# A decoder layer on one core: experts on tiles of 256 slots with stationary split weights, and one logarithm-and-exponential piece fewer in the attention

## The reference

```python
x = x + attention(layernorm(x))          # 16 heads, width 64 each for Q, K, V and the gate G
#   W = (1e-4 + cdist(Q, K)) ** -2 ;  W = W / (1e-4 + W.sum(-1))
#   H = G * (W @ V) ;  H @ W_out + b_out
x = x + cross_attention(layernorm(x), ctx)   # 16 heads, 77 keys, masked softmax
# experts on z = layernorm(x):
#   y = rmsnorm(z) ; top 2 of 8 experts by y @ gate_w ; softmax over the two
#   h = silu(y @ W1[e]) * (y @ W2[e])    # 256 -> 704, twice
#   out = h @ W3[e]                      # 704 -> 256
#   x = x + z + sum over the two experts of weight * out
```

## Time and profile before

| | before |
|---|---|
| time, median of 3 (us) | 1433.6 (1432.44 to 1435.71) |
| profiled execution: time, span (us) | 1438.0, 1436.2 |
| mean granted clock of PE | 0.957 |
| PE busy | 1293.2 us, 90% |
| DVE busy | 1131.8 us, 79% |
| ACT busy | 1036.1 us, 72% |
| POOL busy | 681.1 us, 47% |

### The profile page before, as it was taken

How to read it: one execution, slowest core, us unless ns; L and a number is a source line. 1 busy time by engine, 2 the same in 40 slices (tenths; PEclk the granted TensorE clock), 3 DMA queues, 4 the chain that set the end, 5 groups by cost and what they waited for, 6 DMA issues and landing times.

```text
span 1436.2 us, 23659 instructions
## 1 busy us (share of the span) xinstructions
PE 1293.2 (90%) x7065; PEld 862.1 (60%) x7066; DVE 1131.8 (79%) x1707; ACT 1036.1 (72%) x882; POOL 681.1 (47%) x516
## 2 busy tenths in 40 slices
PE   5899999999999999999997946999992999999995
PEld 4545554555455455545553714888872888888884
DVE  6988988898889889988988473788877767666672
ACT  1699999999999999999999921333332465656552
POOL 5456556665665665566555052333331244434441
PEclk9999999999999999999999768999995999999998
DMA  5000000000000000000000034122220144323322
GB/s 155 2 14 16 30 15 29 15 22 22 16 28 15 29 15 29 15 29 15 22 15 23 7 113 131 52 66 61 63 98 18 27 132 115 75 51 93 93 37 73
DMA packets 68830, 67.25 MB, mean 47 GB/s; under 512 B 6752, under 2 KB 61280, under 8 KB 68768
## 3 DMA queue, kind: packets, MB, share of 16 engines
q1 hardware_dynamic: 61504, 56.91, 12.4%
q0 software_dynamic: 7296, 9.97, 4.1%
HBM read 49.03 MB, written 19.92 MB: 48 GB/s over the span
## 4 chain that ended last, share of the span: by engine, by line
PE 50%; ACT 19%; issue 15%; DVE 12%; DMA 2%; POOL 1%; DVEq 0%; POOLq 0%; ACTq 0%; SPq 0%
ACT wts L1581 11%; PE ps_s L853 10%; PE ps_s L582 8%; PE ps_o L878 7%; PE ps_o L598 5%; PE ps_p L493 4%; PE ps_o L671 4%; ACT wts L1583 4%; DVE wts L1053 4%; PE ps_s L704 2%; PE ps_p L866 2%; PE ps_s L732 2%; ACT L1578 1%; PE ps_o L689 1%; PE ps_s L484 1%
## 5 line engine op out<-in xcount | busy, mean ns | idle before, releaser
L1053 DVE TENSOR_SCALAR wts<-ps_s,k 128x1024 f32<-128x1024 f32 x240 | 296.9, 1279 | 55.9 <-PE ps_s L582 52.5
L1760 POOL TENSOR_TENSOR v_aug<-v_aug,wts 128x1024 f32<-128x1024 f32 x96 | 232.4, 2421 | 228.0 <-DVE v_aug L1042 227.6
L598 PE MATMUL ps_o<-wts,head_rows 128*64 128x512 f32 x1024 | 249.0, 610 | 3.6 <-ACT wts L1583 3.6
L1581 ACT ACTIVATE wts<-wts,eps_d 128x2048 f32<-128x2048 f32 (+1 forms) x96 | 246.0, 2562 | 0.2
L1575 ACT ACTIVATE wts<-wts 128x4096 f32<-128x4096 f32 (+1 forms) x80 | 230.1, 2931 | 22.1 <-DVE wts L1061 19.1
L1583 ACT ACTIVATE wts<-wts 128x2048 f32<-128x2048 f32 (+1 forms) x96 | 238.4, 2484 | 3.0
L582 PE MATMUL ps_s<-q_hi,k_hi 64*128 64x512 f32 x512 | 122.8, 473 | 34.0 <-DVE wts L1053 17.8
L598 PEld LDWEIGHTS ps_o<-wts,head_rows 128*64 128x64 f32 x1024 | 63.3, 137 | 128.0 <-issue 117.6
L1042 DVE TENSOR_TENSOR v_aug<-v_aug,wts 128x1024 f32<-128x1024 f32 x96 | 126.5, 1318 | 6.5 <-ACT wts L1583 6.1
L878 PE MATMUL ps_o<-wts 128*128 x456 | 112.2, 388 | 0.7 <-DVE wts L1496 0.7
L582 PEld LDWEIGHTS ps_s<-q_hi,k_hi 64*128 64x128 f32 x512 | 49.2, 185 | 103.4 <-DVE wts L1053 62.4
(11 more groups left out here) (279 smaller groups left out, 2920.5 us busy)
## 6 DMA issues: line engine op xcount, KB each, us to landing
wts<-in_w SPq DMA_DIRECT2D x16, 704.0 KB
raw<-in_w_in SPq DMA_DIRECT2D x64, 128.0 KB, 2.2
h_t<-o_raw SPq DMA_DIRECT2D x16, 512.0 KB, 2.7
head_rows<-h_t SPq DMA_DIRECT2D x16, 512.0 KB, 4.3
wts<-in_w SPq DMA_DIRECT2D x8, 640.0 KB
acc<-wts SPq DMA_DIRECT2D x17, 128.0 KB, 1.9
wts<-in_x SPq DMA_DIRECT2D x2, 1024.0 KB, 5.8
wts<-in_x SPq DMA_DIRECT2D x1, 2048.0 KB, 9.3
```

Of the source, the lines that this page charges most:

```text
L598: mm = pe.matmul(ps_o[r, t], v_pair[:, b, r], wts[:, h, b, t], start=b == 0, stop=b == SB - 1)
L1053: dve.tensor_scalar(wts[:, h, b, :], ps_s[:, h, :], k2[:, 2 * b + h:2 * b + h + 1], 0.0, ALU.add, ALU.max).then_inc(S_.max_ok, 1)
L1581: act.activation(chunk(start, end), chunk(start, end), ACT.Ln, bias=eps_d[:, 0:1]).then_inc(S_.ln_ok, 1)
L1760: pool.tensor_tensor(acc_w[:, 0], acc_w[:, 0], wts[:, 0, b], ALU.add).then_inc(S_.add_ok, 1)
```

## The change

**Attention.** LOGS joins blocks 2 and 3 into one piece, so ACT runs four activations of 4096 elements a partition for blocks 2 to 7 and two pairs of 2048 for blocks 0 and 1; `rows_inverse` stands behind the joined piece.

**Experts.** A tile has 256 slots (TT), so there are 2, 2, 2, 3, 4, 2, 2 and 3 tiles, 20 in all, run one after the other. The weights' parts become the stationary operand (128 columns of a weight) and the turned y, 256 slots, moves. The products then come out with the hidden width on partitions, so h is not turned: `turn_h` and its copies go. A tile has 66 products for up and gate in three steps (g = 0, 1: two 128-wide pieces of the width each; g = 2: the fifth piece, and the last 64 of up and gate together), and 36 for down: h and W3 are also split into two parts (three products each), where before there was a single f32 product. All have 256 moving columns. ACT makes the high parts of h (`high_hidden`) and W3 (`high_down`), DVE the low parts (`low_hidden`, `low_down`). The weights' parts have one buffer, renewed in three pieces behind the steps of the tile before. `weigh_slots` is 768 wide a part in place of 640; its second half, PE's sum (`slot_weights`) and `read_slot_weights` stand inside tiles 0 and 1. POOL reads and writes two halves per tile; k_step shares a buffer with o_raw (o_step).

```diff
-LOGS = ((0, 1), (1, 2), (2, 3), (3, 4), (4, 6), (6, 8))
+LOGS = ((0, 1), (1, 2), (2, 4), (4, 6), (6, 8))
...
+ET = NT + E
+ES = 2 * ET
+TT = 2 * P
...
+        y_hi, y_lo = (v[:].rearrange("p (a c t) -> p a c t", a=2, c=DC) for v in (q_hi, q_lo))
...
+            def turn_in(k, n):
+                for q in (S_.yg_even, S_.yg_odd):
+                    pe.wait_ge(q, 16 * (k + 1))
+                if n >= 1:
+                    pe.wait_ge(S_.ytt_ok, 2 * k)
+                for half in range(2):
+                    for c in range(DC):
+                        mm = pe.transpose(ps_o[:, c * TT + half * P:c * TT + (half + 1) * P], y_in[:, half, c * P:(c + 1) * P], ident)
+                mm.then_inc(S_.yt2_mm, 1)
+            def hidden(k, out, weights):
                 for c in range(DC):
...
+                    y = [v[:, bass.ds(k & 1, 1), c].rearrange("p a t -> p (a t)") for v in (y_hi, y_lo)]
+                    w_hi, w_lo = (w(c) for w in weights)
+                    for n, (w, y_part) in enumerate(((w_hi, y[0]), (w_lo, y[0]), (w_hi, y[1]))):
+                        mm = pe.matmul(out, w, y_part, start=n == c == 0, stop=n == 2 and c == DC - 1)
+                return mm
...
+            def up_gate(k, g, n):
+                if g == 0:
+                    pe.wait_ge(S_.ytt_ok, 2 * k + 2)
+                pe.wait_ge(S_.wlo_ok, W_PIECES * k + g + 1)
+                if n >= 1:
+                    pe.wait_ge(S_.hm_ok, W_PIECES * (k - 1) + g + 1)
+                if g < 2:
+                    for j in range(2):
+                        for kind in range(2):
+                            out = ps_s[:, g, kind * HALF + j * TT:kind * HALF + (j + 1) * TT]
...
+                else:
+                    for kind in range(2):
+                        hidden(k, ps_p[:, kind * HALF:kind * HALF + TT], [lambda c, w=w: w[:, kind, c] for w in w_fifth])
+                    mm = hidden(k, ps_p[:, TT:2 * TT], [lambda c, w=w: w[:, c].rearrange("p k n -> p (k n)") for w in w_both])
...
+            def down(k, n):
+                pe.wait_ge(S_.hlo_ok, 2 * k + 2)
+                pe.wait_ge(S_.w3l_ok, k + 1)
+                if n >= 1:
+                    pe.wait_ge(S_.o_ok2, 2 * k)
...
+                        w_hi, w_lo = (w3_short if j == NC - 1 else [w[:, j] for w in w3_long])
+                        for m, (h, w) in enumerate(((h_hi, w_hi), (h_hi, w_lo), (h_lo, w_hi))):
+                            mm = pe.matmul(out, h, w, start=at == m == 0, stop=m == 2 and at == NC - 1)
+                mm.then_inc(S_.w3_mm, 1)
...
+            def expert_tile(k, n, last=False):
+                up_gate(k, 0, n)
+                if not last:
+                    turn_in(k + 1, n + 1)
+                if n == 1:
+                    slot_weights()
+                up_gate(k, 1, n)
                 if n >= 1:
-                    turn_h(i - 1, 1 - par, n == 1)
-                pe.wait_ge(S_.e_in, count)
-                pe.wait_ge(S_.ytt_ok, 2 * i + 2)
-                up_gate(i, par, 0, n == 0)
-                up_gate(i, par, 1, n == 0)
-                if not last:
-                    if n >= 2:
+                    if n == 1:
                         pe.wait_ge(S_.wslot_ok, 3)
-                    turn_in(i + 1, 1 - par, k + par)
-                if n >= 1:
-                    down(i - 1, 1 - par, slot_of(i - 1), n == 1)
+                    down(k - 1, n - 1)
+                up_gate(k, 2, n)
...
+                dve.tensor_copy(hi, ps_o[:, 0:HALF]).then_inc(S_.ytt_ok, 1)
+                dve.wait_ge(S_.ytt_ok, 2 * k + 1)
+                dve.tensor_tensor(lo, ps_o[:, 0:HALF], hi.bitcast(F32), ALU.subtract).then_inc(S_.ytt_ok, 1)
...
+            def gated(k, g, n):
+                dve.wait_ge(S_.silu_ok, W_PIECES * k + g + 1)
+                if n >= 1:
+                    dve.wait_ge(S_.hlo_ok, 2 * (k - 1) + (2 if g == 2 else 1))
+                if g < 2:
+                    dve.tensor_tensor(h_all[:, 2 * g:2 * g + 2].rearrange("p n t -> p (n t)"), s_up[g], ps_s[:, g, HALF:],
+                                      ALU.mult).then_inc(S_.hm_ok, 1)
+                else:
+                    dve.tensor_tensor(h_all[:, 4], s_up[2][:, 0:TT], ps_p[:, HALF:HALF + TT], ALU.mult)
+                    dve.tensor_tensor(h_all[DEL:P, 5], s_up[2][DEL:P, TT:], ps_p[DEL:P, TT:2 * TT], ALU.mult).then_inc(S_.hm_ok, 1)
...
+            def low_hidden(k, part):
+                dve.wait_ge(S_.hh_ok, 2 * k + part + 1)
+                hi, lo = (h_four, h_two)[part]
+                dve.tensor_tensor(lo, h_all[:, 4 * part:min(4 * part + 4, NC)], hi.bitcast(F32), ALU.subtract).then_inc(S_.hlo_ok, 1)
+            def expert_tile(k, n, last=False):
+                slot = slot_of(k)
                 if not last:
-                    slot = slot_of(i + 1)
-                if n >= 1:
-                    copy_h(i - 1, 1 - par, n - 1)
+                    slot_next = slot_of(k + 1)
+                gated(k, 0, n)
                 if not last:
-                    low_parts(i + 1, 1 - par, slot, 0, DC)
-                gated(i, par, 0, n)
+                    copy_in(k + 1)
+                    low_parts(k + 1, slot_next, 0)
+                if n == 1:
+                    read_slot_weights()
+                gated(k, 1, n)
                 if not last:
-                    low_parts(i + 1, 1 - par, slot, DC, 2 * DC)
-                gated(i, par, 1, n)
+                    low_parts(k + 1, slot_next, 1)
+                if n == 0:
+                    weigh_slots(1)
+                low_hidden(k, 0)
+                gated(k, 2, n)
+                low_down(k, slot)
+                low_hidden(k, 1)
                 if not last:
-                    copy_in(i + 1, 1 - par, n + 1)
+                    low_parts(k + 1, slot_next, 2)
...
-                    if c == 3 and not first:
+                    if c == 2 and not first:
                         rows_inverse(n - 1)
...
+                else:
+                    act.activation(s_up[2][:, 0:TT], ps_p[:, 0:TT], ACT.Silu)
+                    act.activation(s_up[2][DEL:P, TT:], ps_p[0:DEL, TT:2 * TT], ACT.Silu).then_inc(S_.silu_ok, 1)
...
+            def high_parts(k, slot, g, n):
+                if n >= 1:
+                    act.wait_ge(S_.ug_mm, W_PIECES * (k - 1) + g + 1)
+                raw12 = w12[:, bass.ds(slot, 1)].rearrange("p s k c n -> p (s k) c n")
+                if g < 2:
+                    high = act.activation(w_wide[0][g], raw12[:, :, :, g * TT:(g + 1) * TT], ACT.Copy)
+                else:
+                    act.activation(w_fifth[0], raw12[:, :, :, 4 * P:5 * P], ACT.Copy)
+                    high = act.activation(w_both[0].rearrange("p c k n -> p k c n"), raw12[:, :, :, 5 * P:], ACT.Copy)
+                high.then_inc(S_.whi_ok, 1)
...
+            def high_down(k, slot, n):
+                if n >= 1:
+                    act.wait_ge(S_.w3_mm, k)
+                raw3 = w3_sb[:, bass.ds(slot, 1)].rearrange("p s n d -> p (s n) d")
+                act.activation(w3_long[0], raw3[:, 0:NC - 1], ACT.Copy)
+                act.activation(w3_short[0], raw3[DEL:P, NC - 1], ACT.Copy).then_inc(S_.w3h_ok, 1)
+            def high_hidden(k, part, n):
+                act.wait_ge(S_.hm_ok, W_PIECES * k + (3 if part else 2))
+                if n >= 1:
+                    act.wait_ge(S_.w3_mm, k)
+                act.activation((h_four, h_two)[part][0], h_all[:, 4 * part:min(4 * part + 4, NC)], ACT.Copy).then_inc(S_.hh_ok, 1)
...
+            def copy_out(k, n):
+                act.wait_ge(S_.w3_mm, k + 1)
                 act.wait_ge(S_.wslot_ok, 3)
-                act.activation(o_sb[:, par], ps_o[:, HALF:HALF + D], ACT.Copy, scale=w_slot[:, bass.ds(i, 1)]).then_inc(S_.o_ok2, 1)
...
+            def expert_tile(k, n, last=False):
+                slot = slot_of(k)
+                if not last:
+                    slot_next, count = slot_of(k + 1), count_of(k + 1)
+                silu(k, 0, n)
+                if not last:
                     act.wait_ge(S_.e_in, count)
-                    if not (isinstance(i, int) and i <= 1):
...
+                    high_parts(k + 1, slot_next, 0, 1)
+                silu(k, 1, n)
                 if not last:
-                    slot, count = slot_and_count(i + 1)
+                    high_parts(k + 1, slot_next, 1, 1)
                 if n >= 1:
-                    copy_h(i - 1, 1 - par, n - 1)
+                    copy_out(k - 1, n - 1)
+                high_hidden(k, 0, n)
+                silu(k, 2, n)
+                high_down(k, slot, n)
+                high_hidden(k, 1, n)
                 if not last:
-                    high_parts(i + 1, 1 - par, slot, count, 0, DC)
...
+            def fetch_tile(k):
+                for half in range(2):
+                    fetch(k, half, 1)
+            def put_tile(k, first=False):
+                for half in range(2):
+                    put(k, half, first)
+            fetch_tile(1)
```

(33 more changed lines are left out.)

352 lines of the change are left out of this document (125 added, 227 removed).

## The result

| | before | changed |
|---|---|---|
| time, median (us) | 1434.03 (4 runs, 1432.44 to 1435.71) | 1446.41 (4 runs, 1444.29 to 1448.37) |
| ratio, 95% interval | | 1.0075, 1.0061 to 1.0090 |
| profiled execution: time, span | 1438.0, 1436.2 | 1444.29, 1442.0 |

The prediction was 1424, faster; the time rose by 12.4 us.

What follows compares the result with a forecast made beforehand. PE was taken to bound the experts; in the attention ACT's own work tied with the loop through ACT, DVE and PE. Experts -24.1 and attention +14.6 gave -9.5, so 1433.6 became 1424 us, range 1405 to 1441.

Steps and rivals of the forecast that it cites:

- The attention's term: Attention: joining blocks 2 and 3 delays DVE's add and lengthens the loop through ACT, DVE and PE; +14.6 us.
- the experts' term: Experts, end to end: 20 tiles of 256 slots at 12.9 us, plus waits at both ends; 24.1 us less.
- +1.15, in 13 of the 15 periods: Attention: us added to each period between pairs by the late add of block 2; first and last counted at 0.
- Rival C: Attention: slack absorbs the later add and ACT's saving of 6.3 us comes through, giving 1403; chance 0.15.
- with slack, since it reads three tiles ahead and writes three behind: Experts, POOL: its round of two reads and two writes, 12.5 to 13.2 us, was taken to have slack.
- rival D: Experts: DVE or POOL, not PE, sets a tile's pace at 13.6 us, giving 1438; chance 0.12.
- first product: Start of the experts: PE's first product waits for both halves of y, at 1116.7 instead of 1112.97.
- The tables of slots: Ahead of PE's wait for the first read: a few DVE instructions, counted at nothing, under 2 us if not covered.
- the first two tiles and the third's first step: Start of the experts: PE's work, slots' sum and waits, including 5.8 us for the slots' weights; 37.0 us.
- 16 tiles at 12.9: Middle of the experts: PE sets the pace, with 102 products of 0.118 us, turns and borders per tile.
- the last `down`: End of the experts: after a wait of 4.8 us, 4.25 us and 1 more at the lower clock.
- Rival B: Experts, PE: weight loads aren't hidden at 256 columns; 1440 at 0.126 us a product, 1459 at 0.135; chance 0.13.

Runs made afterwards that it cites:

- logs_alone: The kernel before the change with only the joined logarithm and exponential piece for blocks 2 and 3 added; 1452.76 us, 1.0117 of the kernel before.
- one_list_copy: The changed kernel with POOL copying the token list of both tile halves in one instruction instead of two; 1435.99 us, 1.0011 of the kernel before.
- logs_undone: The changed kernel with the six separate logarithm and exponential pieces restored, so only the experts differ from before; 1427.70 us, 0.9956 of the kernel before.

## Why the prediction was wrong

The sum was -24.1 for the experts and +14.6 for the attention. Measured apart it is -6.9 and +18. The attention's term held in mechanism; the experts' term failed.

**The attention: right in mechanism, too small.** "+1.15, in 13 of the 15 periods": 13 periods rose by 1.18 to 1.20. The first is as it was (49.01, before 48.96), as forecast. The last, counted at 0, rose by 0.97 (50.09, before 49.12). In the last pair ACT gives back 0.41, as forecast. Together that is 16.2 us, and so the traces have it, from the first table load to the end of the last Exp: 784.15 in place of 767.99. The medians say 18.1 and 18.7; the interval of logs_alone, 14.5 to 19.2, holds 16.2 as well, so the medians' excess can be noise. Rival C is out.

**The experts: the step that failed** is "with slack, since it reads three tiles ahead and writes three behind". Reading ahead hides a delay once; it doesn't shorten a round. The estimate in the same sentence, 12.5 to 13.2, was near the measured 13.50 and already above PE's 12.9 at its upper end. I noted that and let the slack excuse it. This was rival D, at 13.6 us a tile and 1438, given 0.12. The own work of the two others was forecast rightly: ACT 8.9 and DVE 10.6 us a tile, measured 140.17/16 = 8.8 and 165.90/16 = 10.4. Against the trace of the changed kernel, term by term:

- first product, 3.8 forecast for the second half's read: 3.4, for from the first read's issue to the first product it is 8.17 (1120.38 to 1128.55) where it was 4.78. The tables of slots, counted at nothing, put that read 0.8 later: 9.65 behind the start of the routing (1110.73), before 8.86.
- the first two tiles and the third's first step, 37.0 forecast: 35.4. PE's wait for the slots' weights was 5.24, forecast 5.8.
- 16 tiles at 12.9: 220.5 us, 13.78 each, 14.1 us more. Of these 0.1 a tile is PE's own: a product takes 0.120, the upper of the two scalings, not 0.118. Of the other 12.5, 8.7 are waits of PE: for POOL's round, and for the late landings under a weight load, which the sum didn't have at all. The last 3.8 are slower products around these waits (in the 15 us from the longest on, 1329 to 1344, the granted clock is 0.89). one_list_copy got 10.4 back.
- the last `down`, 5.25 forecast: 8.6, since in this trace all of it and not the first part ran at the low clock; its wait 5.66 for 4.8.
- the tiles behind the 16, up to that wait: 0.4 more than forecast; from the last `down` to the end 20.4 for 19.6.

These add up to 18.3 us, which takes the forecast's -24.1 to -5.8; the two traces, from the start of the routing to the end, give 331.3 in place of 336.9, so -5.6. logs_undone's median says -6.9.

**Rival B** (loads not hidden at 256 columns) is out: 0.120 is what 352 columns scaled with a fixed cost gave. The load just covered, by the rule of the Trainium skill, "TensorE: Matmul & The Clock Gate", section "LDWEIGHTS (loading the stationary operand)", is not excluded by that: the trace agrees so far as PE's load queue is busy 12.74 of 13.00 us in a full tile.

The range, 1405 to 1441, ended below the time because its cases were taken one at a time: D at 1438 with the attention as measured, 3.5 dearer, and the last `down` as in this trace, 3.4 dearer, is 1445. (In most other traces that `down` took 6.3 to 7.0 us; with these it is 1443.)
